# Reordering the first round of a two-layer conditioned transformer kernel on one NeuronCore

## The reference

```python
def ada_rmsnorm(x, t, gamma_w, beta_w):                 # per token, scaled and shifted per sequence
    return (t @ gamma_w.T)[:, None] * (x * rsqrt(mean(x * x, -1) + 1e-6)) + (t @ beta_w.T)[:, None]

q, k, v = (split(y @ W.T) for W in (W_q, W_k, W_v))     # y = ada_rmsnorm(x); 16 heads of 16
o = softmax(0.25 * q @ k.T) @ v                         # within one sequence
x2 = x + (t @ attn_alpha_w.T) * (o @ W_o.T)
h = silu(y2 @ gate_w.T) * (y2 @ hidden_w.T)             # y2 = ada_rmsnorm(x2); 1024 hidden features
x3 = x2 + (t @ ffn_alpha_w.T) * (h @ out_w.T + out_b)
out = layernorm(x3) * weight + bias                     # mean and variance per token
out = (out + tanh(t @ lin_w.T + lin_b)) * weight + bias
```

## Time and profile before

| | |
|---|---|
| median of 3 runs | 508.56 us (507.5 to 508.71) |
| the profiled execution | 508.42 us |
| its span | 506.6 us, 11675 instructions |
| PE busy | 478.7 us, 94% |
| DVE busy | 393.4 us, 78% |
| POOL busy | 271.4 us, 54% |
| ACT busy | 241.4 us, 48% |
| chain that ended last | PE 72%, DVE 7%, DMA 5%, ACT 4%, POOL 4%, issue 4% |

### The profile page before, as it was taken

The page is one execution under the profiler, slowest core; times in us unless marked ns, Lnnn a source line. Parts: engine busy times, 40 slices in busy tenths (PEclk is TensorE's granted clock), DMA queues, the critical chain, the costliest instruction groups (busy, mean ns, idle before and its releaser), DMA issues.

```text
span 506.6 us, 11675 instructions
## 1 busy us (share of the span) xinstructions
PE 478.7 (94%) x4456; PEld 400.6 (79%) x4456; DVE 393.4 (78%) x776; ACT 241.4 (48%) x348; POOL 271.4 (54%) x179
## 2 busy tenths in 40 slices
PE   7888989999999999999999999999999999999990
PEld 4666878897878978888888978798788978888890
DVE  5868679778886888878895888878897789685636
ACT  3774743338352653438362563537354484414240
POOL 3447456454269445783269445684259543716471
PEclk9989999999999999999999999999999999999996
DMA  8463370206413082214503073023703062400131
GB/s 190 148 190 118 91 203 12 56 2 165 128 23 85 9 224 58 63 41 126 164 18 86 0 210 80 24 80 85 203 2 103 1 161 48 112 15 8 34 65 61
DMA packets 36058, 44.21 MB, mean 87 GB/s; under 512 B 3136, under 2 KB 31040, under 8 KB 36032
## 3 DMA queue, kind: packets, MB, share of 16 engines
q1 hardware_dynamic: 36032, 43.85, 32.5%
HBM read 35.18 MB, written 4.47 MB: 78 GB/s over the span
## 4 chain that ended last, share of the span: by engine, by line
PE 72%; DVE 7%; DMA 5%; ACT 4%; POOL 4%; issue 4%; SPq 2%; ACTq 0%; DVEq 0%; POOLq 0%
PE banks L645 26%; PE banks L662 16%; PE banks L465 7%; PE banks L563 5%; PE banks L497 4%; PE banks L595 4%; DMA row_b<-rows_dram 3%; PE banks L581 3%; PE banks L586 3%; DVE qpar L1113 1%; PE banks L423 1%; POOL hs L1413 1%; DMA xtok<-x_in 1%; DVE act_t L1185 1%; SPq L312 1%
## 5 line engine op out<-in xcount | busy, mean ns | idle before, releaser
L645 PE MATMUL banks<-x2s,gh 128*128 128x512 f32 x768 | 191.5, 398 | 5.1 <-DVE act_t L1185 4.6
L645 PEld LDWEIGHTS banks<-x2s,gh 128*128 128x128 f32 x768 | 139.9, 188 | 37.7 <-DVE act_t L1185 6.0
L1413 POOL TENSOR_TENSOR hs<-act_t,hs 128x512 fp32r<-128x512 f32 x64 | 83.0, 1301 | 96.0 <-ACT hs L874 96.0
L662 PE MATMUL banks<-wout,hs 128*128 128x256 f32 x768 | 105.1, 286 | 2.2 <-POOL hs L1413 2.1
L662 PEld LDWEIGHTS banks<-wout,hs 128*128 128x128 f32 x768 | 97.8, 188 | 8.1 <-POOL hs L1413 3.1
L874 ACT ACTIVATE hs<-act_t 128x512 fp32r<-128x512 f32 x64 | 40.3, 630 | 92.1 <-DVE act_t L1189 86.1
L867 ACT ACTIVATE act_t<-banks 128x512 f32<-128x512 f32 x64 | 38.2, 597 | 74.9 <-PE banks L645 71.9
L1185 DVE SCALAR_TENSOR_TENSOR act_t<-act_t,banks 128x512 f32<-128x512 f32 x64 | 43.9, 686 | 38.5 <-ACT act_t L867 37.3
L1136 DVE RECIPROCAL work_c<-banks 128x512 f32<-128x512 f32 x16 | 53.7, 3354 | 5.1 <-PE banks L581 5.1
L465 PE MATMUL banks<-xs,wqk 128*128 128x512 f32 x192 | 47.1, 393 | 2.3 <-POOL xs L1365 1.6
L1189 DVE SCALAR_TENSOR_TENSOR act_t<-act_t,banks 128x512 f32<-128x512 f32 x64 | 44.0, 687 | 5.9 <-PE banks L645 1.7
(11 more groups left out here) (118 smaller groups left out, 687.5 us busy)
## 6 DMA issues: line engine op xcount, KB each, us to landing
xtok<-x_in SPq DMA_DIRECT2D x8, 512.0 KB, 5.5
work_c<-xn SPq DMA_DIRECT2D x16, 256.0 KB, 3.5
xres<-x_in SPq DMA_DIRECT2D x8, 512.0 KB, 7.1
row_aa<-rows_dram SPq DMA_DIRECT2D x16, 256.0 KB, 6.7
row_af<-rows_dram SPq DMA_DIRECT2D x16, 256.0 KB, 5.9
row_b<-rows_dram SPq DMA_DIRECT2D x16, 256.0 KB, 6.4
shift<-rows_dram SPq DMA_DIRECT2D x16, 256.0 KB, 6.1
y<-final SPq DMA_DIRECT2D x7, 512.0 KB, 3.2
```

The source lines that it names most:

```text
L645: last = mm(banks[:, base + part, :], gh[:, a, k, w:w + P], x2s[:, b, k, :], start=(n == 0), stop=(n == 5))
L662: last = mm(banks[:, t // 2, D * (t % 2):D * (t % 2) + D], hs[:, c % 2, b, P * t:P * t + P], wout[:, a, c, :], start=(c == 0 and a == b an ...
L1413: tt(hs[:, c % 2, 1, :], act_t[:, c % 2, :], hs[:, c % 2, 0, :].bitcast(F32), ALU.subtract)\
```

## The change

Four lists of the first round are reordered and two numbers changed.

- ACT: `keep_v(0)` goes ahead of `par_k()`, and `cut_hi(3)` from before `place_v_swapped(0)` to behind the second exponential.
- DVE: `setup_weights()` goes from behind `negate_max(0)` to behind `setup_rows()`; the wait for the squares' sums of the second x and `rsqrt_both(1)` go from before `q_out(0)` to behind `negate_max(0)`.
- POOL: `finish_shift()` goes ahead of the scaling of the second x, `o_split(0, 0)` ahead of `cut_lo(5)`, and `cut_lo(6)` behind `xs_split(1)` and a new wait for the four scaled tiles of x2.
- PE: `WARM_MAX` from 4 to 2 and `WARM_OUTPUT` from 16 to 10.

```diff
-WARM_LOADS, WARM_MAX, WARM_OUTPUT, WARM_NORM = 3, 4, 16, 4
+WARM_LOADS, WARM_MAX, WARM_OUTPUT, WARM_NORM = 3, 2, 10, 4
@@ ACT first()
                 pair_q(0)
+                keep_v(0)
                 par_k()
-                keep_v(0)
                 act.wait_ge(zeroed, ZEROED)
                 place_v_kept(0)
                 cut_hi(2)
-                cut_hi(3)
                 place_v_swapped(0)
                 exp(0, 0)
                 exp(0, 1)
+                cut_hi(3)
                 cut_hi(4)
@@ DVE first()
                 setup_rows()
+                setup_weights()
                 dve.wait_ge(stage_lo, 1)
                 stats_x(1, x2n)
-                dve.wait_ge(x_stats, XS * 2)
-                rsqrt_both(1)
                 q_out(0)
                 for n in range(4):
                     max_over_keys(0, n)
                 negate_max(0)
-                setup_weights()
+                dve.wait_ge(x_stats, XS * 2)
+                rsqrt_both(1)
                 normalise(0, 0)
@@ POOL first()
                 cut_lo(1)
+                pool.wait_ge(x_stats, XS * 2)
+                finish_shift()
                 pool.wait_ge(norm1_steps, RS * 2)
                 tt(xtok[:, :, :], xtok[:, :, :], nt1[:, 1, 0, :].unsqueeze(2).to_broadcast([P, TT, D]),
                    ALU.mult).then_inc(xs_scaled, 1)
-                finish_shift()
                 cut_lo(2)
                 cut_lo(3)
                 cut_lo(4)
+                o_split(0, 0)
                 cut_lo(5)
-                o_split(0, 0)
                 o_split(0, 1)
+                xs_split(1)
+                pool.wait_ge(x2n_scaled, TT)
                 cut_lo(6)
-                xs_split(1)
```

## The result

| | median, 20 runs each | range |
|---|---|---|
| before | 508.54 us | 507.5 to 509.54 |
| changed | 511.03 us | 508.26 to 514.3 |

The changed kernel takes 1.0051 times the time of the one before (95% interval 1.0037 to 1.0065). That is 2.5 us more where 2.2 less was forecast, and the time lies outside the stated range. The runs of changed spread over 6 us, those of before over 2 in these twenty; in later sets before itself reached 512.9. The profiled execution took 511.04 us with a span of 509.1.

A forecast was written before the change was run, and what follows sets the result against it. TensorE bounds the loop, so a gain must come from the first round's chain of waits: 1.35 us at the first exponential, 1.6 with o_split, 2.2 with cut_lo(6). 508.42 - 2.2 = 506.2 us, range 504.9 to 508.4, forecast's chance 0.58.

The forecast's parts named there:

- keep_v ahead of par_k: ACT, first round: keep_v ends 2.6 us earlier, so v's exchange lands at 27.85, not 30.48; par_k ends 0.3 later.
- setup_weights: DVE, first round: two products moved to 15.98 fit an idle 0.79 us; counted, with finish_shift, at nothing.
- first sum: First round: first exponential at 30.45 instead of 31.81 us, 1.35 earlier, set by TensorE and no longer by v.
- clock, one stretch more: Rival: TensorE's gaps keep the clock low 3.4 us longer, scores cost 1.7 more, 507.9 us; chance 0.18.
- slower: Rival: clock low through both attends, to about 38 us, costs 4.5 for a gain of 2.2, 510.7 us; chance 0.09.
- POOL's order: POOL: o_split ahead of cut_lo(5) gains 0.25 us; cut_lo(6) behind the second x's lo part brings the final sum to 2.2.
- The Newton chain: DVE: ten instructions moved behind negate_max, 2.0 us from about 28.9 to 31.0, hidden; q_out starts 0.9 earlier.
- The gain persists through the loop: Loop, seven of eight groups: bound by TensorE and untouched, so a first-round gain survives, rows shifted by 2.2 us.

The follow-up runs named there:

- old warm-ups: Changed kernel with the warm-up numbers of the kernel before (WARM_MAX 4, WARM_OUTPUT 16): 512.02 us, ratio to before 1.0074.
- both moves in before: Kernel before with only keep_v put ahead of par_k and setup_weights behind setup_rows: 510.88 us, ratio to before 1.0055.
- rows held: Changed kernel with one SP wait holding load_aa and the stage load behind it until the first attend is done: 507.98 us, ratio 0.999.
- only load_aa held: Changed kernel with stage load 7 let through and only load_aa held on SP until the first attend is done: 508.71 us, ratio 0.9987.
- both: Changed kernel with WARM_MAX 4, WARM_OUTPUT 16, and load_aa and the stage load held until the first attend is done: 508.09 us, ratio 1.0004.
- filled: Changed kernel, load_aa and stage load held, warm-ups into v's bank around the third score group, 12 ahead of o_proj: 505.78 us, ratio 0.9936.
- filled, not held: The filled kernel without the SP wait in front of load_aa: 504.77 us, ratio to before 0.9933.
- POOL's order of before: The filled kernel with the old POOL order of o_split, cut_lo(5), cut_lo(6) and xs_split(1): 506.23 us, ratio to before 0.9961.
- Newton chain back: The filled kernel with the Newton chain of the second x back ahead of q_out: 507.16 us, ratio to before 0.9986.
- warm-ups alone: Kernel before with only the warm-ups reduced, 4 to 2 and 16 to 10: 508.71 us, ratio to before 1.0017.
- setup_weights alone: Kernel before with only setup_weights moved behind setup_rows on DVE: 508.56 us, ratio to before 1.0008.
- keep_v alone: Kernel before with only keep_v moved ahead of par_k on ACT: 509.76 us, ratio to before 1.0048.

## Why the prediction was wrong, step by step

*keep_v ahead of par_k*, together with *setup_weights*, is the step that failed. The forecast saw that all that stands behind v's exchange in SP's queue goes "2.6 or more earlier", and put this and the move of `setup_weights` at nothing. Its own queue order had the row table's reads in it; what they would meet was not asked. It also misread what held the table's store: in the kernel before SP waited 3.5 us for DVE there, behind the exchange, so that with `keep_v` alone the reads stay at 35.5, and only both moves bring them to 32.8. In its place the runs showed a standstill of TensorE of 2.3 to 3.1 us; holding the reads takes back the whole loss (ratio 1.0051 to 0.999). The runs (us; the fetch is the second one of TensorE's first round):

| kernel | `load_aa` issued | first attend starts | fetch starts | standstill |
|---|---|---|---|---|
| before | 35.3 | 34.2 | 36.3 | none |
| changed | 32.3 | 34.4 | 41.2 | 3.1 |
| old warm-ups | 31.8 | 34.9 | 40.8 | 2.3 |
| both moves in before | 32.8 | 35.5 | 41.7 | 2.6 |
| rows held | 37.6 | 35.5 | 36.6 | none |
| only load_aa held | 37.8 | 35.8 | 36.9 | none |
| both | 34.7 | 32.6 | 33.6 | none |
| filled | 33.7 | 31.6 | 32.8 | none |
| filled, not held | 32.2 | 31.8 | 32.8 | none |
| POOL's order of before | 33.7 | 31.7 | 33.2 | none |
| Newton chain back | 35.9 | 33.8 | 34.8 | none |
| warm-ups alone | 34.1 | 33.4 | 35.3 | none |
| setup_weights alone | 35.1 | 33.8 | 35.7 | none |
| keep_v alone | 35.5 | 35.3 | 36.7 | none |

With nothing in flight (rows held, both) the fetch comes 1.0 to 1.1 us after the first attend starts, with plain loads in flight 1.0 to 2.1 us after it. Where `load_aa` was issued more than 2 us ahead of that attend, it comes 6.0 to 6.8 us after it, and TensorE runs dry. In all three of these kernels the fetch starts 0.01 us behind the last packet of the other queue, that is, when not only the reads but also the stage load behind them are through. That the early reads delay the fetch is shown by taking them away and putting them back. By what path they do it is not: the trace doesn't say which DMA engines carried either, nor when a fetch was asked for.

The Trainium skill has the pieces. "Runtime: NRT & Kernel Launch", section Instruction fetch mechanics, says that an engine's instructions come in blocks of 16 KiB through a DMA queue of its sequencer while the current block runs; the trace agrees (16 KB packets, kind "instruction"). "DMA: Bandwidth & Descriptors", section Queues, rings and completion order, says that a DMA engine takes turns between its queues packet by packet. By that rule the fetch would wait for one packet; here it came about 5 to 6 us late, and the measurement decides.

*Warm-ups and the first sum.* `keep_v` ran at 22.34 and the exchange had landed by 27.6, as forecast; the scores started at 28.52, earlier than the forecast 29.03. But the clock stayed low until 33.2, and the sum of 1.35 came out as -0.14 at the third scores. This was the rival "clock, one stretch more", priced at 1.7 and measured at 1.6; it was given 0.18, and it is what the runs mostly do. Its reason was wrong, though: the clock fell at 26.3, ahead of the pauses behind the maximum, and with the old number of warm-ups it fell in the same way. What the runs point to are the two gaps of 1.1 us ahead of the fall. The second score group followed the first at once, as forecast, but the third waits for the first maximum and started only 0.44 us earlier; the idle time was put into one piece. The kernel with the gaps filled is 2.2 us faster than with the rows held (507.98 to 505.78, different sets), 2.9 faster than with only `load_aa` held (508.71, the same set), and none of its runs had more than 12 us of low clock. That the gaps and not the other edits of that run do this is argued, not shown.

The rival "slower" had 510.7 for its price, close to the measured 511.03, but by luck: it had the clock low through both attends, to about 38, and here it was back at 33.2. The rest is the standstill, which no rival had.

*Together.* The rivals held one cost each; what hurt was that the two feed each other. The low clock delayed TensorE's request past the issue of the loads, and the standstill let the clock fall again.

*POOL's order.* Right in kind: without the standstill and with the clock full `xs_split(1)` released the K projection at 48.57, forecast 48.6. Taken alone it was worth 1.2 us in the profile of its experiment, where 0.85 was forecast. In the changed kernel it bound nothing. The new wait of `cut_lo(6)` cost 0.75 there, since x2 was scaled only at 58.4: the forecast had 0.3 us between the cut's end and `beta_x2`, and nothing on what happens when x2n is later than TensorE.

*The Newton chain* was right in place and size (2.0 us, done at 30.3, hidden); *setup_weights* fitted its gap on DVE (15.80 to 16.55), though what it set free on SP was not nothing. *The gain persists through the loop*: right, with the other sign.

## What to carry to other kernels

- A transfer that starts earlier is not free: ask what else will want the DMA engines then, and count the engines' own instruction fetches in. An idle time put down to "issue" in straight-line code, with a late packet of the kind "instruction" at its end, is this case.
- Put warm-ups into the gaps ahead of the work whose speed matters, and into a bank that makes them wait for nothing; behind the gaps twice as many left the fall of the clock as long here (6.8 us in both profiles).
- When one kernel's runs spread over several microseconds, sort them by granted clock before averaging: here the same code took 505 or 509 us. It doesn't explain all: two runs of before with only 7 us of low clock took 509.4 and 510.0.

## What the runs showed of the hardware that was not expected

- The fetch of 16 KB starts 1.0 to 1.1 us behind the first attend's start when nothing is in flight, 1.0 to 2.1 us behind it beside plain loads or just ahead of the row table's reads, and 6.0 to 6.8 us behind it when the reads (two transfers of 256 KB each, 64 destination partitions from each source row) and the stage load behind them were issued more than 2 us before that attend; then it starts as their last packet does.
- In the changed kernel the granted clock fell after a stretch in which TensorE was busy 0.93 of 2 us in bursts of 0.4 to 0.6 us; in the profile of the run "Both" the same 0.93 of 2 us came and the clock held. The falls of the first round lasted 3.4 us (before), 6.8 (changed) and 10.2 (rows held). In three profiles (keep_v alone, only load_aa held, Newton chain back) it was also low once from 13.7 or 13.9 us for 3.4 us, in a stretch that these edits don't touch.
- The time of the same kernel mostly followed its low-clock time: in the run "Both" 505.0 us at 7 us low, 509.5 at 19.
